# Spreading the sort of the group after next over the steps of a group, one operation at a time

## The chip, the cores and the metric

The program runs on one core of a Trainium2 chip. The metric is the device time of one launch in microseconds (us). TensorE is called PE here, VectorE DVE, ScalarE ACT, GpSimd POOL and SyncE SP. Each of them runs its own instruction stream in order; semaphores tie the streams together.

## The reference: a graph layer, an attention block and a mixture of experts

The input is `x` (3125 nodes by 256 features), 53125 edges (`src`, `dst`, `edge_weight`) and the weights of three blocks:

```python
xn = _layernorm(x)
x = x + gnn(xn, src, dst, edge_weight, W, b) + mix(xn, ...)   # mix: linear attention, 8 heads, two MLP layers
x = x + ffn(_layernorm(x), ...)                               # ffn: 16 experts, top 2 of them per token
# gnn:
msgs = edge_val[:, None] * x[edge_col]
agg = segment_sum(msgs, edge_row, num_segments=3125)
out = agg @ W.T + b
```

The change lies in the graph part alone: each edge takes the row of its `src` node, scales it by its weight and adds it to its `dst` node. Everything is float32.

## The kernel before

The kernel has five stages: norm of `x` with keys and a projection of every node written to the DRAM tensor `y_rows` (to about 170 us of the span); the edges, in 13 groups (to about 862 us); the dense attention block; the routing of tokens to experts; and the experts. The change touches the second stage.

**A group.** The edges lie in 416 columns of 128 partitions, so 13 groups (`NG`) of `GE` = 32 columns, 4096 edges each. The 3125 nodes are 25 bins (`BINS`) of 128. A group's edges are first sorted by bin, which gives `GT` = 32 tiles of 128 edges; then POOL gathers the tile's 128 rows of `y_rows` by an indirect DMA for each tile (`gather`, L582); then a group is added up in `STEPS` = 56 steps. Steps 0 to 31 are the tiles (variable `t`). Steps 32 to 55 (variable `b`, from 0 to 23) are the 24 borders between bins, where a tile belongs to two of them. Below they are called row steps and border steps, and a step number counts through both, so step 35 is `b == 3`.

**A step.** DVE makes a one-hot matrix `hot` for the step four further on (`LEAD` = 4; `hot_row` L1064, `hot_cross` L1069); PE multiplies it by the gathered rows into PSUM (L733, L748, two matmul instructions a step); DVE adds the result to `agg` (`evict_row` L1076 at each row step; `evict_pair` L1082 for two border steps at once). An eviction waits for PE by the semaphore `met` and for the eviction before it by `evicted`. PE waits for `hot_ready`. A PSUM bank holds two steps, and four banks take turns. Register values that say which bin and which column a step has are loaded by `TENSOR_LOAD` instructions on DVE at steps 0 and 16 (L1091) and 28 (L1095), and on PE after step 31 (L739).

**The sort beside it.** While group g is added up, DVE and PE also sort group g+2. It is written by hand where in the steps this happens. On DVE:

- after step 2, `count_bins`: `in_bin` (L954, 128x800) and a running count over it (L958);
- after step 16, `find_places`: adds PE's prefix sums (L963), masks (L967), reduces to a place for each edge (L972) and splits the place into tile and slot (L974 to L977);
- after steps 22, 26, 35 and 43, `make_records(g+2, k)` for the quarters k = 0 to 3 (`CH` = 8 columns each): `in_tile` (L982) and three fields of `record` (L988);
- after step 55, `make_list`: copies the sorted list out of PSUM and releases POOL's gather.

On PE: `prefix` after the matmul of step 12 (L646 to L649), and `reorder(g+2, k)`, eight products of `in_slot` and `record` (L658, sixteen matmul instructions), after the matmuls of steps 28, 34, 42 and 50. A reorder waits for its records and for ACT's `in_slot` (`slot_hot`, L392 and L394), which waits for the places.

A `drain` on DVE holds the next instruction until those before it have written. The last two groups (11 and 12) have no sort beside them, since there are no groups 13 and 14.

Of the kernel before, what the change touches and what calls it, by code (L numbers as in the profile page):

```python
# [5 lines left out]
ALU = mybir.AluOpType  # L6
# [9 lines left out]
P = 128  # L16
# [6 lines left out]
def gps_layer(nc, x, src, dst, edge_weight, gnn_W, gnn_b, Wq, Wk, Wv, Wm, W1, W2, g1, b1, g2, b2,  # L23
# [42 lines left out]
    with ExitStack() as ctx:  # L66
# [553 lines left out]
        def _(pe):  # L620
# [102 lines left out]
            def add_up(g):  # L723
                h = g % 2
                pe.wait_ge(list_ready, g + 1)
                for t in range(GT):
                    n = g * STEPS + t
                    if t % GC == 0:
                        pe.wait_ge(gathered[h][t // GC], 16 * GC * (g // 2 + 1))
                    pe.wait_ge(hot_ready, n + 1)  # L730
                    if t % 2 == 0 and g * UNITS + t // 2 >= RING:
                        pe.wait_ge(evicted, evictions_before(g, t // 2))
                    pe.matmul(bank_of(g, t // 2)[:, (t % 2) * C:(t % 2 + 1) * C], hot[:, n % HOTS, :], rows[h][:, t, :],  # L733
                              start=True, stop=True).then_inc(met, 1)
                    if g + 2 < NG and t == 12:
                        prefix(g + 2)
                    if g + 2 < NG and t == 28:
                        reorder(g + 2, 0)
# [184 lines left out]
        def _(dve):  # L923
# [25 lines left out]
                last.then_inc(xn_ready, 1)  # L949

            def count_bins(g):

                dve.tensor_tensor(in_bin[:, :, :], edges_of(bin_f, g).unsqueeze(1).to_broadcast([P, BINS, GE]),  # L954
                                  iota[:, 0:BINS].unsqueeze(2).to_broadcast([P, BINS, GE]), ALU.is_equal)
                dve.drain()
                flat = in_bin[:, :, :].rearrange("p b c -> p (b c)")
                dve.tensor_tensor_scan(count[:, 1:1 + BINS * GE], flat, flat, 0.0, ALU.add, ALU.max).then_inc(counts_ready, 1)  # L958

            def find_places(g):  # L960
                dve.wait_ge(prefix_ready, g + 1)
                places = count[:, 1:1 + BINS * GE].rearrange("p (b c) -> p b c", c=GE)
                dve.scalar_tensor_tensor(places, cross_before.unsqueeze(2).to_broadcast([P, BINS, GE]), -1.0, places,  # L963
                                         ALU.add, ALU.add)
                dve.tensor_copy(ends[:, :], ends_col)
                dve.drain()
                dve.tensor_tensor(places, places, in_bin[:, :, :], ALU.mult)  # L967

                dve.tensor_scalar(meets[:, :], tile_start[:, :], ends[:, 0:1], None, ALU.is_ge)
                dve.drain()  # L970
                with nc.allow_low_precision(reason="each sum is one whole number and zeros"):
                    dve.tensor_reduce(place_i[:, 0, :], places.rearrange("p b c -> p c b"), AX, ALU.add)  # L972
                dve.drain()
# [5 lines left out]
            def make_records(g, k):  # L979
                own = slice(k * CH, (k + 1) * CH)  # L980
                dve.drain()
                dve.tensor_tensor(in_tile[:, :, :], place_i[:, 1, own].unsqueeze(2).to_broadcast([P, CH, GT]),  # L982
                                  iota[:, 0:GT].unsqueeze(1).to_broadcast([P, CH, GT]), ALU.is_equal)
                dve.drain()
                if g * CHUNKS + k >= 2:
                    dve.wait_ge(reordered, g * CHUNKS + k - 1)
                for f in range(FIELDS):
                    last = dve.tensor_tensor(record[k % 2][:, :, f, :], in_tile[:, :, :],  # L988
                                             edges_of(edge[:, f, :], g, k).unsqueeze(2).to_broadcast([P, CH, GT]), ALU.mult)
                last.then_inc(record_ready, 1)  # L990

            def make_list(g):
                h = g % 2
# [84 lines left out]
            def evict_pair(g, a):  # L1078
# [2 lines left out]
                dve.wait_ge(evicted, g * EVICTS + GT + a)  # L1081
                dve.tensor_tensor(own, bank_of(g, GT // 2 + a), own, ALU.add).then_inc(evicted, 1)  # L1082

            def add_up(g):
                h = g % 2
                if g == 0:
# [2 lines left out]
                for t in range(GT):  # L1089
# [357 lines left out]
```

## Time and profile before

| | us |
|---|---|
| median of 3 runs | 1557.48 (1555.85 to 1558.01) |
| the profiled execution, its own time | 1554.42 |
| its span in the trace | 1552.6 |
| PE busy | 1207.1 (78%) |
| DVE busy | 960.4 (62%) |
| POOL busy | 574.9 (37%) |
| ACT busy | 357.6 (23%) |
| granted PE clock over the span | 0.919 of full speed |

The groups with a sort take 54.4 to 54.9 us each once the pipeline runs (groups 2 to 10); group 0 takes 66.5, group 1 57.0, and groups 11 and 12 together 73.3. Shares over the whole span mix five stages; what the change can move is read inside a group, from the order of DVE's and PE's instructions in time and from what each idle stretch ended with.
### The profile page before, as it was taken

To read this page: it belongs to the slowest core of one execution; us is meant where nothing else is said; L and a number is where in the kernel's file an instruction comes from. 1 tells how busy PE (TensorE), PEld (TensorE's weight loads), DVE (VectorE), ACT (ScalarE), POOL (GpSimd) and SP (SyncE) were. 2 spreads that over 40 slices of the span, in tenths; PEclk is the share of its full clock that TensorE was granted. 3 is DMA by queue.
4 is the path that set the end of the run, shared out by engine and by line. 5 is a ranking of instruction groups with operands and counts; after the bars stand their busy time and mean duration, and the time that the engine had idled before them with its cause. 6 is when DMAs were issued, how large, how long until landed. Compare 5 with 4: busy or idle time off the path is not lost.

```text
span 1552.6 us, 24067 instructions
## 1 busy us (share of the span) xinstructions
PE 1207.1 (78%) x7172; PEld 1010.1 (65%) x7172; DVE 960.4 (62%) x2681; ACT 357.6 (23%) x881; POOL 574.9 (37%) x587
## 2 busy tenths in 40 slices
PE   0589776776677677677789999999239999999990
PEld 0466455654565465455544888998229999999990
DVE  2962388888888888888989565544752222222225
ACT  0455231132033113203300343334111111111110
POOL 1420477657447545644752000000033333333320
PEclk9889987998999899899899999999559999999995
DMA  3211233323223222322321000000058999999967
GB/s 118 67 35 34 71 104 104 94 79 92 66 68 101 68 69 82 89 65 69 104 69 43 1 1 17 17 17 17 15 180 292 332 334 331 336 331 332 335 219 254
DMA packets 118265, 196.07 MB, mean 126 GB/s; under 512 B 13421, under 2 KB 67499, under 8 KB 118187
## 3 DMA queue, kind: packets, MB, share of 16 engines
q1 hardware_dynamic: 92074, 123.82, 24.0%
q0 software_dynamic: 26112, 71.34, 14.8%
q8 instruction: 33, 0.54, 0.1%
q14 instruction: 46, 0.37, 0.1%
HBM read 177.12 MB, written 17.99 MB: 126 GB/s over the span
## 4 chain that ended last, share of the span: by engine, by line
PE 58%; DVE 22%; issue 6%; DVEq 6%; DMA 3%; POOL 2%; SPq 2%; ACT 1%; ACTq 0%; POOLq 0%
PE psum L891 15%; PE psum L733 8%; PE psum L901 7%; PE psum L748 6%; PE psum L799 6%; PE psum L658 5%; DVE agg L1076 4%; PE psum L807 3%; DVE agg L1082 2%; DVE record L988 2%; PE psum L679 2%; POOL arena L582 2%; DVE in_tile L982 2%; DVE hot L1064 2%; DVEq L1091 1%
## 5 line engine op out<-in xcount | busy, mean ns | idle before, releaser
L582 POOL DMA_INDIRECT arena<-y_rows,gather_i x416 | 403.0, 969 | 334.3 <-DVEq L1011 131.5
L733 PE MATMUL psum<-arena,hot 128*128 128x256 f32 x832 | 265.8, 461 | 142.1 <-DVE hot L1064 83.2
L733 PEld LDWEIGHTS psum<-arena,hot 128*128 128x128 f32 x832 | 169.1, 224 | 228.5 <-DVE hot L1064 126.3
L392 ACT ACTIVATE in_slot<-iota,place_f 128x128 f32<-128x128 f32 x416 | 126.9, 387 | 450.8 <-DVE place_f L977 398.9
L748 PE MATMUL psum<-arena,hot 128*128 x624 | 161.8, 395 | 38.5 <-DVE hot L1069 35.1
L1076 DVE TENSOR_TENSOR agg<-psum,agg 128x256 f32 x416 | 175.9, 423 | 18.2 <-PE psum L733 17.2
L891 PEld LDWEIGHTS psum<-arena 128*128 128x128 f32 x1536 | 181.1, 194 | 4.9 <-issue 2.5
L891 PE MATMUL psum<-arena 128*128 128x128 f32 x1536 | 181.6, 277 | 1.9 <-DVE arena L1373 1.9
L1380 DVE TENSOR_TENSOR arena<-psum,arena 128x512 f32<-128x512 f32 x64 | 44.3, 692 | 202.8 <-PE psum L891 202.8
L748 PEld LDWEIGHTS psum<-arena,hot 128*128 128x128 f32 x624 | 109.0, 190 | 80.7 <-issue 70.9
L1064 DVE TENSOR_SCALAR hot<-iota,node_in_bin,weight 128x128 f32<-128x128 f32 x416 | 145.1, 354 | 24.3 <-issue 24.2
L605 POOL DMA_INDIRECT chosen_rows<-arena,back_at x64 | 63.2, 987 | 219.7 <-DVE arena L1387 215.0
L595 POOL TENSOR_TENSOR xnT<-xnT,token 128x1600 bf16<-128x1600 bf16 x2 | 10.5, 5271 | 302.2 <-DVE xnT L1349 302.2
L1082 DVE TENSOR_TENSOR agg<-psum,agg 128x512 f32<-128x512 f32 x156 | 106.5, 682 | 20.4 <-PE psum L748 20.2
L658 PE MATMUL psum<-record,in_slot 128*128 128x96 f32 x832 | 107.3, 285 | 13.2 <-DVE record L988 13.2
L524 ACT ACTIVATE arena<-psum 128x512 f32<-128x512 f32 x64 | 38.2, 597 | 335.0 <-PE psum L891 335.0
L658 PEld LDWEIGHTS psum<-record,in_slot 128*128 128x128 f32 x832 | 105.0, 201 | 15.9 <-DVE record L988 13.6
L1069 DVE TENSOR_SCALAR hot<-iota_all,node,weight 128x128 f32<-128x128 f32 x312 | 97.5, 349 | 8.2 <-issue 8.1
L901 PE MATMUL psum<-arena 128*128 128x256 f32 x384 | 90.9, 380 | 0.0
L901 PEld LDWEIGHTS psum<-arena 128*128 128x128 f32 x384 | 69.3, 191 | 7.3
L600 POOL DMA_INDIRECT xnT<-n_rows,token_of x64 | 62.0, 969 | 28.7 <-issue 18.9
L988 DVE TENSOR_TENSOR record<-in_tile,edge 128x256 f32<-128x256 f32 x156 | 64.6, 470 | 3.9
(199 smaller groups left out, 1608.3 us busy)
## 6 DMA issues: line engine op xcount, KB each, us to landing
arena<-in_L_ffn_w_dram SPq DMA_DIRECT2D x144, 512.0 KB, 5.7
xnT<-in_L_ffn_w_dram SPq DMA_DIRECT2D x48, 512.0 KB
arena<-y_rows,gather_i POOLq DMA_INDIRECT x416, 2.8
arena<-chosen_rows SPq DMA_DIRECT2D x8, 640.0 KB, 9.1
agg<-in_x_dram SPq DMA_DIRECT2D x4, 640.0 KB, 11.1
y_rows<-arena SPq DMA_DIRECT2D x4, 640.0 KB, 3.4
n_rows<-arena SPq DMA_DIRECT2D x4, 640.0 KB
out_dram<-agg SPq DMA_DIRECT2D x4, 640.0 KB
```

Of the source, the lines that this page charges most:

```text
L392: act.activation(in_slot[k % 2][:, c, :], iota[:, :], ACT.Abs, bias=place_f[:, k * CH + c:k * CH + c + 1])
L582: pool.indirect_dma_start(rows[h][:, t, :], None, y_rows, bass.IndirectOffsetOnAxis(ap=gather_i[h][:, t:t + 1], axis=0)).then_inc(gathered ...
L658: last = pe.matmul(in_order, in_slot[k % 2][:, c, :], record[k % 2][:, c, :, :].rearrange("p f t -> p (f t)"), start=(k == 0 and c == 0), ...
L733: pe.matmul(bank_of(g, t // 2)[:, (t % 2) * C:(t % 2 + 1) * C], hot[:, n % HOTS, :], rows[h][:, t, :], start=True, stop=True).then_inc(met, 1)
L748: pe.matmul(bank_of(g, unit)[:, (b % 2) * C:(b % 2 + 1) * C], hot[:, n % HOTS, :], rows[h][:, bass.ds(row_of[b], 1), :].rearrange("p t c - ...
L891: last = pe.matmul(bank[b][:, m * P:(m + 1) * P], w[s][:, k * EH + m * P:k * EH + (m + 1) * P], e_xT[:, h, k * P:(k + 1) * P], start=(k == ...
L901: last = pe.matmul(bank[6 + h][:, 0:C], e_hid[:, h, k * P:(k + 1) * P], e_w3[s][:, k * C:(k + 1) * C], start=(k == 0), stop=(k == EHC - 1))
L988: last = dve.tensor_tensor(record[k % 2][:, :, f, :], in_tile[:, :, :], edges_of(edge[:, f, :], g, k).unsqueeze(2).to_broadcast([P, CH, GT ...
L1064: dve.tensor_scalar(hot[:, n % HOTS, :], iota[:, :], node_in_bin[g % 2][:, t:t + 1], weight[g % 2][:, t:t + 1], ALU.is_equal, ALU.mult).th ...
L1069: dve.tensor_scalar(hot[:, n % HOTS, :], iota_all[:, (b + 1) * P:(b + 2) * P], node[g % 2][:, bass.ds(col, 1)], weight[g % 2][:, bass.ds(c ...
L1076: dve.tensor_tensor(own, bank_of(g, t // 2)[:, (t % 2) * C:(t % 2 + 1) * C], own, ALU.add).then_inc(evicted, 1)
L1082: dve.tensor_tensor(own, bank_of(g, GT // 2 + a), own, ALU.add).then_inc(evicted, 1)
```

## The change

The operations of the sort are the same, and so are their number, shapes and drains. They are cut into seven kinds of pieces, and each piece is issued after a step of its own, in `sort_beside(g, step)`. PE's `prefix` moves from step 12 to step 10.

```diff
-                    if g + 2 < NG and t == 12:
+                    if g + 2 < NG and t == 10:
                         prefix(g + 2)
...
-            def count_bins(g):
-
+            def mark_bins(g):
                 dve.tensor_tensor(in_bin[:, :, :], edges_of(bin_f, g).unsqueeze(1).to_broadcast([P, BINS, GE]),
                                   iota[:, 0:BINS].unsqueeze(2).to_broadcast([P, BINS, GE]), ALU.is_equal)
-                dve.drain()
+
+            def count_marks(g):
                 flat = in_bin[:, :, :].rearrange("p b c -> p (b c)")
+                dve.drain()
                 dve.tensor_tensor_scan(count[:, 1:1 + BINS * GE], flat, flat, 0.0, ALU.add, ALU.max).then_inc(counts_ready, 1)
...
+            def add_prefix(g):
                 dve.wait_ge(prefix_ready, g + 1)
...
+            def make_field(g, k, f):
+                if f == 0:
+                    dve.drain()
+                    if g * CHUNKS + k >= 2:
+                        dve.wait_ge(reordered, g * CHUNKS + k - 1)
+                last = dve.tensor_tensor(record[k % 2][:, :, f, :], in_tile[:, :, :],
+                                         edges_of(edge[:, f, :], g, k).unsqueeze(2).to_broadcast([P, CH, GT]), ALU.mult)
+                if f == FIELDS - 1:
+                    last.then_inc(record_ready, 1)
...
+            def sort_beside(g, step):
+                if step == 1:
+                    mark_bins(g)
+                if step == 3:
+                    count_marks(g)
+                if step == 13:
+                    add_prefix(g)
+                if step == 15:
+                    mask_places(g)
+                if step == 17:
+                    sum_places(g)
+                if step == 19:
+                    split_places(g)
+                for k, first in enumerate((20, 25, 34, 42)):
+                    if step == first:
+                        mark_tiles(g, k)
+                    if first < step <= first + FIELDS:
+                        make_field(g, k, step - first - 1)
...
                     if g + 2 < NG:
-                        if t == 2:
-                            count_bins(g + 2)
-                        if t == 16:
-                            find_places(g + 2)
-                        if t in (22, 26):
-                            make_records(g + 2, (t - 22) // 4)
+                        sort_beside(g + 2, t)
...
-                    if g + 2 < NG and b in (3, 11):
-                        make_records(g + 2, 2 + b // 8)
+                    if g + 2 < NG:
+                        sort_beside(g + 2, GT + b)
```

`mask_places`, `sum_places` and `split_places` hold the rest of `find_places` in its old order, each with the drain that stood in front of it; `mark_tiles` holds the drain and the `in_tile` operation of `make_records`.

In the rows below, `hot` is the one-hot matrix, `agg<-psum,agg` an eviction, and ISA an instruction of the sequencer alone.

**DVE, around step 16.** Before, the load of step 16 stands behind an eviction, and all of `find_places` behind the eviction of step 16:

```order
L1076 ISA
L1076 TENSOR_TENSOR agg<-psum,agg 128x256
L1091 TENSOR_LOAD bin_of
L1064 TENSOR_SCALAR hot<-iota,node_in_bin,weight 128x128
L1076 ISA
L1076 TENSOR_TENSOR agg<-psum,agg 128x256
L963 SCALAR_TENSOR_TENSOR count<-psum,count 128x800
L965 COPY ends<-psum 25x1
L967 TENSOR_TENSOR count<-count,in_bin 128x800
L969 TENSOR_SCALAR meets<-tile_start,ends 25x32
L972 TENSOR_REDUCE place_i<-count 128x32
L974 TENSOR_SCALAR place_i<-place_i 128x32
```

Now the same place, from the eviction of step 15 on:

```order
L1099 TENSOR_TENSOR agg<-psum,agg 128x256
L971 TENSOR_TENSOR count<-count,in_bin 128x800
L972 TENSOR_SCALAR meets<-tile_start,ends 25x32
L1133 TENSOR_LOAD bin_of
L1087 TENSOR_SCALAR hot<-iota,node_in_bin,weight 128x128
L1099 ISA
L1099 TENSOR_TENSOR agg<-psum,agg 128x256
L1087 TENSOR_SCALAR hot<-iota,node_in_bin,weight 128x128
L1099 ISA
L1099 TENSOR_TENSOR agg<-psum,agg 128x256
L977 TENSOR_REDUCE place_i<-count 128x32
```

The masking operation has moved ahead of the load, the prefix addition two steps further ahead, and the reduction one step behind it.

**DVE, around the load of step 28.** Before, the three fields of quarter 1, a one-hot matrix and an eviction stand ahead of it:

```order
L982 TENSOR_TENSOR in_tile<-place_i,iota 128x256
L988 TENSOR_TENSOR record<-in_tile,edge 128x8x32 x3
L1064 TENSOR_SCALAR hot<-iota,node_in_bin,weight 128x128
L1076 ISA
L1076 TENSOR_TENSOR agg<-psum,agg 128x256
L1095 TENSOR_LOAD cross_col
```

Now the second field stands right ahead of it, and the third behind the step:

```order
L1005 TENSOR_TENSOR record<-in_tile,edge 128x8x32
L1087 TENSOR_SCALAR hot<-iota,node_in_bin,weight 128x128
L1099 ISA
L1099 TENSOR_TENSOR agg<-psum,agg 128x256
L1005 TENSOR_TENSOR record<-in_tile,edge 128x8x32
L1137 TENSOR_LOAD cross_col
L1092 ISA
L1092 TENSOR_SCALAR hot<-iota_all,node,weight 128x128
L1099 ISA
L1099 TENSOR_TENSOR agg<-psum,agg 128x256
L1005 TENSOR_TENSOR record<-in_tile,edge 128x8x32
```

Two of the three fields stay ahead of the load, with the step 27 between them.

**DVE, border steps 34 to 36 (b = 2 to 4), quarter 2.** Here `in_tile` and the fields stand one by one:

```order
L997 TENSOR_TENSOR in_tile<-place_i,iota 128x256
L1092 ISA
L1092 TENSOR_SCALAR hot<-iota_all,node,weight 128x128
L1105 TENSOR_TENSOR agg<-psum,agg 128x512
L1005 TENSOR_TENSOR record<-in_tile,edge 128x8x32
L1092 ISA
L1092 TENSOR_SCALAR hot<-iota_all,node,weight 128x128
L1005 TENSOR_TENSOR record<-in_tile,edge 128x8x32
```

Before, they stood as one row of four operations behind the eviction of step 35, as the block in front of the load above does. On PE only `prefix` has moved, by two steps.

## Rows read from the trace of the kernel before

**Rows 1.** The chain of work that ended last, the page: shares by engine.

```profile
PE 58%; DVE 22%; issue 6%; DVEq 6%; DMA 3%; POOL 2%; SPq 2%; ACT 1%; ACTq 0%; POOLq 0%
```

**Rows 2.** Windows, group 2, groups 11 with 12: length, busy us, PEclk, DMA.

```profile
297.50:351.90 54.40, 39.67 (x186) 30.29 (x186) 48.32 (x138) 13.90 (x36) 31.00 (x32) 0.91 0.26 78
...
789.10:862.40 73.30, 64.32 (x216) 33.97 (x216) 66.83 (x196) 0.00 (x0) 30.50 (x32) 1.00 0.20 58
```

**Rows 3.** DVE by line, groups 2 to 10: count | busy, mean ns | idle before.

```profile
L1076 DVE TENSOR_TENSOR agg<-psum,agg 128x256 f32 x288 | 121.7, 423 | 5.4 <-PE psum L733 4.6 <-issue 0.5 <-PE psum L748 0.2
L1064 DVE TENSOR_SCALAR hot<-iota,node_in_bin,weight 128x128 f32<-128x128 f32 x288 | 100.0, 352 | 18.1 <-issue 18.1
L1082 DVE TENSOR_TENSOR agg<-psum,agg 128x512 f32<-128x512 f32 x108 | 73.8, 683 | 16.5 <-PE psum L748 16.5
```

**Rows 4.** DVE in time, group 5, step 15 to find_places: start, us, operation.

```profile
475.88 0.42 DVE L1076 TENSOR_TENSOR agg<-psum,agg 128x256 f32 x1
477.05 0.34 DVE L1064 TENSOR_SCALAR hot<-iota,node_in_bin,weight 128x128 f32<-128x128 f32 x1 [0.75 <-issue]
...
478.76 0.99 DVE L967 TENSOR_TENSOR count<-count,in_bin 128x800 f32<-128x800 f32 x1
```

**Rows 5.** DVE in time, step 28's load, group 5; then group 12.

```profile
490.71 1.10 DVE L988 TENSOR_TENSOR record<-in_tile,edge 128x256 f32<-128x256 f32 x3
491.73 0.34 DVE L1064 TENSOR_SCALAR hot<-iota,node_in_bin,weight 128x128 f32<-128x128 f32 x1
491.98 0.41 DVE L1076 TENSOR_TENSOR agg<-psum,agg 128x256 f32 x1
492.82 0.43 DVE L1069 TENSOR_SCALAR hot<-iota_all,node,weight 128x128 f32<-128x128 f32 x1 [0.42 <-issue]
...
847.10 0.34 DVE L1069 TENSOR_SCALAR hot<-iota_all,node,weight 128x128 f32<-128x128 f32 x1 [1.36 <-issue]
```

**Rows 6.** PE in time, group 5, steps 40 to 47 with reorder 2.

```profile
500.63 1.80 PE L748 MATMUL psum<-arena,hot 128*128 x6 [1.10 <-DVE hot L1069]
502.27 1.92 PE L658 MATMUL psum<-record,in_slot 128*128 128x96 f32 x16
504.03 2.35 PE L748 MATMUL psum<-arena,hot 128*128 x10
```

**Rows 7.** DVE in time, group 5, steps 35 to 43.

```profile
498.62 0.43 DVE L982 TENSOR_TENSOR in_tile<-place_i,iota 128x256 f32<-128x256 int32 x1
499.12 1.09 DVE L988 TENSOR_TENSOR record<-in_tile,edge 128x256 f32<-128x256 f32 x3
...
501.76 0.68 DVE L1082 TENSOR_TENSOR agg<-psum,agg 128x512 f32<-128x512 f32 x1
...
502.88 0.68 DVE L1082 TENSOR_TENSOR agg<-psum,agg 128x512 f32<-128x512 f32 x1
...
504.69 0.69 DVE L1082 TENSOR_TENSOR agg<-psum,agg 128x512 f32<-128x512 f32 x1 [0.63 <-PE psum L748]
```

**Rows 8.** DVE in time, group 5, one row step with nothing beside it.

```profile
488.77 0.34 DVE L1064 TENSOR_SCALAR hot<-iota,node_in_bin,weight 128x128 f32<-128x128 f32 x1
489.06 0.42 DVE L1076 TENSOR_TENSOR agg<-psum,agg 128x256 f32 x1
```

**Rows 9.** ACT in time, group 5: in_slot of quarters 0 and 1.

```profile
482.14 2.44 ACT L392 ACTIVATE in_slot<-iota,place_f 128x128 f32<-128x128 f32 x8 [36.02 <-DVE place_f L977]
...
485.62 2.43 ACT L392 ACTIVATE in_slot<-iota,place_f 128x128 f32<-128x128 f32 x8
```

**Rows 10.** PE in time, group 0, step 28.

```profile
213.69 0.70 PE L733 MATMUL psum<-arena,hot 128*128 128x256 f32 x2 [1.26 <-DMA arena<-y_rows,gather_i]
```

**Rows 11.** Windows: group 0, then group 5 at steps 5 to 9 and 28 to 43.

```profile
196.00:202.00 6.00, 4.53 (x12) 3.03 (x10) 3.51 (x10) 0.00 (x0) 4.64 (x5) 0.50 0.36 109
469.00:472.00 3.00, 2.72 (x6) 2.19 (x7) 3.00 (x11) 0.00 (x0) 2.10 (x3) 0.50 0.35 104
...
491.00:503.00 12.00, 9.73 (x56) 7.87 (x56) 10.66 (x32) 7.01 (x18) 8.52 (x9) 1.00 0.34 105
```

More of the change, by code:

```diff
@@ L949, in x_norm @@
                 last.then_inc(xn_ready, 1)
-            def count_bins(g):
+            def mark_bins(g):
                 dve.tensor_tensor(in_bin[:, :, :], edges_of(bin_f, g).unsqueeze(1).to_broadcast([P, BINS, GE]),
                                   iota[:, 0:BINS].unsqueeze(2).to_broadcast([P, BINS, GE]), ALU.is_equal)
+            def count_marks(g):
+                flat = in_bin[:, :, :].rearrange("p b c -> p (b c)")
                 dve.drain()
-                flat = in_bin[:, :, :].rearrange("p b c -> p (b c)")
                 dve.tensor_tensor_scan(count[:, 1:1 + BINS * GE], flat, flat, 0.0, ALU.add, ALU.max).then_inc(counts_ready, 1)
-            def find_places(g):
+            places = count[:, 1:1 + BINS * GE].rearrange("p (b c) -> p b c", c=GE)
+            def add_prefix(g):
                 dve.wait_ge(prefix_ready, g + 1)
-                places = count[:, 1:1 + BINS * GE].rearrange("p (b c) -> p b c", c=GE)
                 dve.scalar_tensor_tensor(places, cross_before.unsqueeze(2).to_broadcast([P, BINS, GE]), -1.0, places,
@@ L965, in find_places, with mask_places @@
                 dve.tensor_copy(ends[:, :], ends_col)
+            def mask_places(g):
                 dve.drain()
@@ L969, in find_places, with sum_places @@
                 dve.tensor_scalar(meets[:, :], tile_start[:, :], ends[:, 0:1], None, ALU.is_ge)
+            def sum_places(g):
                 dve.drain()
@@ L972, in find_places, with split_places @@
                     dve.tensor_reduce(place_i[:, 0, :], places.rearrange("p b c -> p c b"), AX, ALU.add)
+            def split_places(g):
                 dve.drain()
@@ L977, in find_places, with count_bins, mark_tiles @@
                 dve.tensor_scalar(place_f[:, :], place_i[:, 2, :], -1.0, None, ALU.mult).then_inc(places_ready, 1)
-            def make_records(g, k):
+            def count_bins(g):
+                mark_bins(g)
+                count_marks(g)
+            def find_places(g):
+                for part in (add_prefix, mask_places, sum_places, split_places):
+                    part(g)
+            def mark_tiles(g, k):
                 own = slice(k * CH, (k + 1) * CH)
@@ L983, in make_records @@
                                   iota[:, 0:GT].unsqueeze(1).to_broadcast([P, CH, GT]), ALU.is_equal)
-                dve.drain()
-                if g * CHUNKS + k >= 2:
-                    dve.wait_ge(reordered, g * CHUNKS + k - 1)
+            def make_field(g, k, f):
[7 more added lines that the diff above has]
+                    last.then_inc(record_ready, 1)
+            def make_records(g, k):
+                mark_tiles(g, k)
                 for f in range(FIELDS):
-                    last = dve.tensor_tensor(record[k % 2][:, :, f, :], in_tile[:, :, :],
-                                             edges_of(edge[:, f, :], g, k).unsqueeze(2).to_broadcast([P, CH, GT]), ALU.mult)
-                last.then_inc(record_ready, 1)
+                    make_field(g, k, f)
             def make_list(g):
@@ L1082, in evict_pair @@
                 dve.tensor_tensor(own, bank_of(g, GT // 2 + a), own, ALU.add).then_inc(evicted, 1)
+            def sort_beside(g, step):
+                if step == 1:
+                    mark_bins(g)
+                if step == 3:
+                    count_marks(g)
+                if step == 13:
[8 more added lines that the diff above has]
+                    if step == first:
+                        mark_tiles(g, k)
+                    if first < step <= first + FIELDS:
+                        make_field(g, k, step - first - 1)
             def add_up(g):
```

## The prediction

> **What bounds the kernel now.** I read the chain of work first, then the windows by group, then DVE's idle time by line, then DVE and PE in time. The chain [rows 1] names PE for 58% and DVE for 22%, but over five stages; it doesn't say which is short inside a group. The windows do [rows 2]: the nine groups 2 to 10 lie between 297.50 and 789.10, 54.6 us each, and in the one shown DVE is busy 48.3 and PE 39.7. DVE is the full engine. What a faster order can win is therefore DVE's idle time and nothing of its work. In those nine groups [rows 3] it idles 16.5 us in border evictions and 4.8 in row evictions, each time for PE, that is 1.83 and 0.53 us a group; and 18.1 us (2.0 a group) ahead of a one-hot matrix for "issue", which is the two L1091 loads. The sum is some 4.4 us a group, and of that the load at step 0 stands behind `make_list`, which isn't touched. Groups 11 and 12, without a sort, take 36.65 each, so the sort costs 18 us a group, nearly all of it DVE's own work that stays.
>
> PE's idle stretches beside `find_places` look like the large thing but cost nothing themselves: PE catches up, a step taking it 0.47 us (5 steps in 2.35 [rows 6]) and DVE 0.63 (0.34 from eviction to one-hot, 0.29 back [rows 5, 8]). They cost only through what is late after them.
>
> **The load of step 16.** It follows an eviction that starts at 475.88; the next one-hot matrix starts at 477.05 [rows 4], 1.17 later instead of 0.34, so 0.83 us are exposed and the load takes about 1.1. In the new order the masking operation (0.99) and a short one stand ahead of it, and the sequencer can take the load while they run. If it needs about 0.1 to hand over the two, the one-hot matrix starts 1.3 after the masking operation's start, where the engine is free at 1.04: 0.26 exposed. Gain 0.57. The bounds are 0 (the load waits for the engine) and 0.83.
>
> **The load of step 28.** Before, the block starts at 490.71 and the next one-hot matrix at 492.82, though the engine could take it at 492.32: 0.50 exposed. In group 12, with no block ahead, the row shows 1.36 idle [rows 5]. The block thus gives the sequencer a lead of 0.9. After, only one field, a step and another field stand behind the last drain. If the sequencer's hand-over sets the load's start, it starts about 0.35 after the first field and the matrix follows 2.14 after it, the engine being free at 1.28: 0.86 exposed, a loss of 0.36. If it was the number of instructions ahead in the queue, nothing is lost. I take 0.17, halfway. Both loads together: +0.40 a group.
>
> **The border evictions.** Before, the four operations of a quarter hold DVE from 498.62 on (0.50 to the first field, then 0.34 for each, with 0.18 for the drain in front 1.7 in all), PE has no one-hot matrix for 1.10 us, runs three steps, then reorders for 1.76 (502.27 to the next start at 504.03) [rows 6, 7]. The eviction of steps 42 and 43 comes 1.81 after the one before it, not 1.12, and waits 0.63. The reorder itself would fit: eight border steps with a quarter's operations cost DVE 4 x 1.11 (two evictions are 1.12 apart) + 1.7 = 6.1, and PE 8 x 0.47 + 1.76 = 5.5. The wait comes from PE's being stopped just before. I lay out the new order at each reorder, counting from the start of the one-hot matrix of the reorder's step. PE: the matrix done and read at 0.4, the step to 1.07 (0.67 for a single one), reorder to 2.83, next step to 3.3, eviction possible at 3.5. DVE reaches that eviction at:
> - quarter 1 (step 34): two row steps 1.27, two border steps 1.11, matrix and drain 0.44, `in_tile` 0.34, matrix 0.26 = 3.42, wait 0.1;
> - quarter 2 (step 42): 2.22 for four border steps, then the same 1.04 = 3.26, wait 0.24;
> - quarter 3 (step 50): no operation is left in these steps, 2.73, wait 0.75.
>
> Sum 1.09 against 1.83: gain 0.74. Bounds: 0, if the waits return elsewhere, and 1.83.
>
> **The row evictions.** Their 0.53 us a group fall in stretches after a block in which PE runs at half clock: 2.72 busy in 3.00 for three steps at a clock of 0.50 (1.2 GHz) [rows 11], slower than DVE's 0.63. The clock had been 1.00 (2.4 GHz), and fell after PE had stood idle beside the counting. PE is now never left without a matrix for longer than one operation and its drain take, where `find_places` held DVE by eight in a row, but the idle stretch around `make_list` is left, and tiles come spaced out. I take half: 0.25, bounds -1.5 (below) and 0.53.
>
> **Instruction overlap.** From one-hot to eviction DVE takes 0.29 in a plain row step, but 0.25 in a step that follows a block [rows 5, 8], since an eviction waits for the end of the one before it and the block has covered that. Fourteen row steps now have an operation ahead of the next matrix instead of four: 10 x 0.04, of which two stand beside loads. 0.25; bounds 0 and 0.4.
>
> **What is not changed.** Same operations and the same drains; a drain behind an eviction costs 0.1 as one behind a short operation does, so 0, with bounds of ±0.3 a group. No DMA moves. ACT now starts its `in_slot` at the end of step 19 instead of 16 and needs 3.5 a quarter (482.14 to 485.62 [rows 9]). PE wants quarter 0 after step 28, when DVE is at step 24: five steps with four operations, 3.2 + 1.7 = 4.9 after the places. It is in time by 1.4, and quarter 1 by 3. The prefix wait at step 13 stands behind a PE step whose matrix was made at step 6. Behind that wait would queue the one-hot matrices of all later steps, so it would hurt if it came; seven steps cover it. `make_list` closes the group as before, so POOL's gathers (31 us busy of 54.5 [rows 2]) keep their cover.
>
> **The sum.** 0.40 + 0.74 + 0.25 + 0.25 = 1.64 us a group, in groups 1 to 10: 16.4. In group 0 the rows come late: PE waits for a gather until 213.69, at step 28 [rows 10], so the row steps gain nothing, and I count the border term alone, 0.7. Together 17.1 off the profiled execution's 1554.4, which gives 1537.3; the shown median stands 3.1 above that execution, so 1540.4.
>
> **Rivals.**
> - *The waits only move* (the new places of the fields leave PE late all the same), or the load of step 28 is exposed at 0.86 or more. For it: reorder 3 keeps its wait in my own layout. Then 0.6 to 0.9 a group stays, 8 us: 1549.
> - *All waits for PE go.* 2.36 + 0.57 + 0.25 = 3.2 in ten groups and 1.8 in group 0, 34 us: 1524. Against it: reorder 3, where nothing delays DVE.
> - *No change*, within 0.2% (3.1 us, about what a measurement can tell here): drains behind evictions eat what the loads give.
> - *Slower: PE's clock.* In group 0, with the tiles paced by the gathers, the clock stood at 0.50 from 196 to 202 [rows 11]. Steps 13 to 19 will be paced similarly by DVE, one in 8.7 / 7 = 1.25 us. If the clock is low when reorders 0 and 1 run, each takes 1.76 longer, and six steps between them 0.3 more than DVE needs: 5.3, less 1.1 of cover, less the 1.64 gained, is 2.6 a group lost, 26 us: 1583. It decides from an extra wait of 1.64, about one reorder at half clock in every group. Against it: border steps with stops of 1.1 us before each reorder keep 1.00 over 491 to 503 [rows 11].
>
> The Trainium skill ("TensorE: Matmul & The Clock Gate", "A second HAM failure mode: psum-queue depth-cycling") tells of a kernel in which short idles between groups of matmuls made the clock oscillate; by that rule many small gaps would be no better than few long ones, and the time would be that of the rival named last. The border steps here speak against it, the gather-paced stretch for it.
>
> **How the numbers follow.** Forecast 0.57 (its own range 1533 to 1546), waits only move 0.19, all go 0.10, no change 0.07, slower 0.07. Faster by over 0.2%: 0.57 + 0.19 + 0.10 = 0.86; same 0.07; slower 0.07. The range 1529 to 1553 holds the first two cases and parts of the next.
>
> **What the changed profile would show.** Groups 2 to 10 of about 53.0 us with DVE busy still 48.3. The idle time ahead of the one-hot matrix at step 16 at 0.2 instead of 0.75, that of step 28 at 0.4 to 0.8. Border evictions waiting 1.1 a group, mostly at step 51. PE with no idle stretch over 2 us but the one around `make_list`. I am wrong if DVE's busy time or its drains grow, if the eviction waits stay near 2.4 a group, if the clock in steps 28 to 36 is below 1.00, or if PE waits for ACT or records at a reorder.

## The result, and the profile after

| | before | after |
|---|---|---|
| median of 10 runs, us | 1556.9 | 1546.06 |
| the profiled execution's span, us | 1552.6 | 1543.0 |
| start of group 0 | 174.0 | 174.9 |
| group 0 | 66.5 | 68.8 |
| group 1 | 57.0 | 54.3 |
| groups 2 to 10, mean | 54.6 | 53.5 |
| granted PE clock over the span | 0.919 | 0.906 |

The changed kernel takes 0.9939 of the time before (95% interval 0.9924 to 0.9953), 9.5 us less. 17.1 were forecast. In the spans the difference is 9.6 us: 0.9 lost ahead of group 0, 2.3 lost in group 0, 2.8 won in group 1, 10.5 won in groups 2 to 10 (1.17 each, where 1.64 was forecast), 0.4 lost behind them. Group times here and below come from one profiled execution of each kernel; that of the changed kernel was one of its two fastest (1544.75; its ten runs lie between 1544.75 and 1552.75).

The groups no longer take the same time. These are the windows of groups 2, 4, 7 and 10 of the changed kernel (length, busy us of PE, its weight loads, DVE, ACT and POOL, PEclk, DMA), which answer to [rows 2]:

```profile
297.90:349.90 52.00, 42.09 (x186) 29.25 (x186) 47.76 (x138) 13.90 (x36) 32.64 (x32) 0.90 0.27 82
...
404.10:457.80 53.70, 44.45 (x186) 31.98 (x186) 47.66 (x137) 13.91 (x36) 32.16 (x32) 0.84 0.27 79
...
563.60:619.00 55.40, 46.41 (x186) 33.68 (x186) 47.94 (x137) 13.91 (x36) 32.88 (x32) 0.82 0.26 76
...
725.90:779.10 53.20, 42.16 (x186) 29.72 (x186) 47.74 (x138) 13.91 (x36) 32.61 (x32) 0.90 0.27 80
```

DVE's work is the same within 0.3 us in all four. The clock differs, but its mean over a group doesn't give the length: groups 2 and 10 both have 0.90 and take 52.0 and 53.2. What gives it is how long DVE waits for PE before its row evictions: nothing in group 2, 1.84 us in group 4, 2.77 in group 7, 0.91 in group 10. With these waits taken off, all nine groups are 51.9 to 52.7 long. Before, the nine lay between 54.4 and 54.9.

DVE by line over groups 2 to 10 of the changed kernel, against [rows 3] (L1099 is L1076 before, L1087 is L1064, L1105 is L1082, L1092 is L1069):

```profile
L1099 DVE TENSOR_TENSOR agg<-psum,agg 128x256 f32 x288 | 121.4, 421 | 11.8 <-PE psum L733 10.5 <-issue 1.4
L1087 DVE TENSOR_SCALAR hot<-iota,node_in_bin,weight 128x128 f32<-128x128 f32 x288 | 99.6, 351 | 12.0 <-issue 11.3
L1105 DVE TENSOR_TENSOR agg<-psum,agg 128x512 f32<-128x512 f32 x108 | 74.2, 687 | 6.3 <-PE psum L748 5.9
L1092 DVE TENSOR_SCALAR hot<-iota_all,node,weight 128x128 f32<-128x128 f32 x216 | 72.7, 360 | 6.9 <-issue 6.9
```

Three of the four went about as laid out: the border evictions wait 6.3 us instead of 16.5, the matrices of the row steps 12.0 instead of 18.1, those of the border steps 6.9 instead of 4.7, for which this is the line of the kernel before:

```profile
L1069 DVE TENSOR_SCALAR hot<-iota_all,node,weight 128x128 f32<-128x128 f32 x216 | 67.5, 349 | 4.7 <-issue 4.5
```

The row evictions went the other way, 11.8 instead of 5.4.

**The loads.** DVE in time in group 2, steps 15 and 16, against [rows 4]:

```profile
313.13 0.99 DVE L971 TENSOR_TENSOR count<-count,in_bin 128x800 f32<-128x800 f32 x1
314.04 0.22 DVE L972 TENSOR_SCALAR meets<-tile_start,ends 25x32 f32<-25x32 f32 x1
314.34 0.35 DVE L1087 TENSOR_SCALAR hot<-iota,node_in_bin,weight 128x128 f32<-128x128 f32 x1
```

The matrix of step 16 starts 1.21 after the masking operation, with less than 0.1 us of idle time: the load runs under the two. And steps 26 to 28, against [rows 5]:

```profile
325.56 0.43 DVE L1005 TENSOR_TENSOR record<-in_tile,edge 128x256 f32<-128x256 f32 x1
325.91 0.34 DVE L1087 TENSOR_SCALAR hot<-iota,node_in_bin,weight 128x128 f32<-128x128 f32 x1
326.16 0.42 DVE L1099 TENSOR_TENSOR agg<-psum,agg 128x256 f32 x1
326.50 0.42 DVE L1005 TENSOR_TENSOR record<-in_tile,edge 128x256 f32<-128x256 f32 x1
327.64 0.35 DVE L1092 TENSOR_SCALAR hot<-iota_all,node,weight 128x128 f32<-128x128 f32 x1 [0.73 <-issue]
```

The matrix follows 2.08 after the first field (2.11 before), with one field less in between, so 0.73 idle instead of 0.42. In the trace the load itself starts 0.32 after that field (0.35 before) and takes 1.60 us both times. It is tied to the field behind the last drain, not to the number of instructions ahead.

**The border steps.** The only wait left in group 2 is the one at reorder 3 [rows 7]:

```profile
343.54 0.69 DVE L1105 TENSOR_TENSOR agg<-psum,agg 128x512 f32<-128x512 f32 x1
344.14 0.60 DVE L1092 TENSOR_SCALAR hot<-iota_all,node,weight 128x128 f32<-128x128 f32 x2
345.35 0.69 DVE L1105 TENSOR_TENSOR agg<-psum,agg 128x512 f32<-128x512 f32 x1 [0.61 <-PE psum L748]
```

**The row steps.** PE in time, group 4, steps 4 to 10 (0 to 3 ran while the group before ended), then DVE's evictions at steps 10 and 12:

```profile
405.75 4.15 PE L733 MATMUL psum<-arena,hot 128*128 128x256 f32 x8 [2.84 <-issue]
411.00 2.90 PE L733 MATMUL psum<-arena,hot 128*128 128x256 f32 x6 [1.10 <-issue]
```

```profile
416.12 0.42 DVE L1099 TENSOR_TENSOR agg<-psum,agg 128x256 f32 x1 [1.45 <-PE psum L733]
417.82 0.42 DVE L1099 TENSOR_TENSOR agg<-psum,agg 128x256 f32 x1 [0.39 <-PE psum L733]
```

And the clock there, in the first 12 us of group 4 and of group 2:

```profile
404.00:416.00 12.00, 9.12 (x25) 6.57 (x26) 9.32 (x24) 0.00 (x0) 9.21 (x9) 0.55 0.28 80
...
298.00:310.00 12.00, 8.81 (x33) 5.68 (x33) 10.69 (x28) 0.00 (x0) 9.30 (x9) 0.86 0.27 82
```

In both groups PE had stood idle 2.8 us beside `make_list`. In group 4 the clock averages 0.55, near its lower level of 0.50, over the 12 us; PE does 25 matmuls in them, in group 2 it does 33. Eight of them take 4.15 us, 1.04 a step, against DVE's 0.63. `prefix`, which now stands behind step 10, comes on top. (A row eviction waits for both steps of its bank, so the one of step 10 waits for the matmuls of step 11, behind `prefix`.) DVE then waits 1.45 and 0.39. In five groups of the nine (3, 4, 6, 7 and 8) these two waits, or a pair like them, stand at steps 10 and 12; group 10 has one of 0.91 at step 10. The kernel before had half clock in the row steps too, but at most 0.9 us of waits for PE in a group.

Group 7 has the dearest case: the clock is low again at step 28, and reorder 0 takes 3.73 instead of 2.02.

```profile
592.15 3.73 PE L658 MATMUL psum<-record,in_slot 128*128 128x96 f32 x16
```

```profile
596.82 0.42 DVE L1099 TENSOR_TENSOR agg<-psum,agg 128x256 f32 x1 [1.87 <-PE psum L733]
```

**Group 0.** PE at step 28, against [rows 10]:

```profile
216.17 0.70 PE L733 MATMUL psum<-arena,hot 128*128 128x256 f32 x2 [1.67 <-DMA arena<-y_rows,gather_i]
216.80 0.40 PE L656 MATMUL psum<-meets,ones 25*128 25x32 f32 x2
217.13 3.38 PE L658 MATMUL psum<-record,in_slot 128*128 128x96 f32 x16
```

The rows come 2.5 us later than before, and the reorder behind them runs at half clock, 3.38 instead of 2.03. Of the 2.5, 0.9 is the later start of the group; the other 1.6 goes with slower gathers on POOL, told under the last heading. But group 0 is not steady between executions, as the kernels of the experiments show. It took 66.9 to 70.3 in the one execution traced of each. Two of them keep the blocks in its row steps, and they took 68.2 and 70.3. The start of the group moved between 174.0 and 176.0, though nothing ahead of it was changed. So one execution of the kernel before, at 66.5, doesn't show that the 2.3 us come from the new order.

### The profile page after: what moved, and what is told of

It reads as the page before. It is cut to its first block, busy times and chain, and to the rows that moved or that the text cites. A ratio compares the mean times of both kernels' runs of the same rounds, so it can differ in the third digit from the quotient of the medians.

```text
span 1543.0 us, 24067 instructions
## 1 busy us (share of the span) xinstructions
PE 1246.6 (81%) x7172; PEld 1018.0 (66%) x7172; DVE 955.8 (62%) x2681; ACT 357.7 (23%) x881; POOL 589.8 (38%) x587
## 4 chain that ended last, share of the span: by engine, by line
PE 57%; DVE 20%; issue 10%; DVEq 5%; DMA 3%; POOL 2%; SPq 2%; ACT 1%; ACTq 0%; POOLq 0%
PE psum L891 15%; PE psum L733 10%; PE psum L901 7%; PE psum L799 6%; PE psum L658 4%; DVE agg L1099 4%; PE psum L748 4%; PE psum L807 3%; DVE hot L1092 3%; DVE agg L1105 2%; PE psum L679 2%; POOL arena L582 2%; DVE hot L1087 1%; DVE record L1005 1%; PE psum L628 1%
## 5 line engine op out<-in xcount | busy, mean ns | idle before, releaser
L582 POOL DMA_INDIRECT arena<-y_rows,gather_i x416 | 417.9, 1005 | 309.1 <-issue 122.8
L733 PE MATMUL psum<-arena,hot 128*128 128x256 f32 x832 | 291.4, 490 | 111.4 <-issue 63.9
L1099 DVE TENSOR_TENSOR agg<-psum,agg 128x256 f32 x416 | 175.5, 422 | 28.3 <-PE psum L733 26.8
L748 PE MATMUL psum<-arena,hot 128*128 x624 | 168.0, 400 | 21.2 <-DVE hot L1092 20.9
L1087 DVE TENSOR_SCALAR hot<-iota,node_in_bin,weight 128x128 f32<-128x128 f32 x416 | 144.6, 353 | 16.9 <-issue 15.7
L595 POOL TENSOR_TENSOR xnT<-xnT,token 128x1600 bf16<-128x1600 bf16 x2 | 10.5, 5270 | 302.4 <-DVE xnT L1386 302.4
L658 PE MATMUL psum<-record,in_slot 128*128 128x96 f32 x832 | 110.9, 291 | 12.7 <-DVE record L1005 12.7
L658 PEld LDWEIGHTS psum<-record,in_slot 128*128 128x128 f32 x832 | 108.4, 207 | 15.4 <-DVE record L1005 13.1
L1105 DVE TENSOR_TENSOR agg<-psum,agg 128x512 f32<-128x512 f32 x156 | 107.1, 687 | 8.0 <-PE psum L748 7.3
L1092 DVE TENSOR_SCALAR hot<-iota_all,node,weight 128x128 f32<-128x128 f32 x312 | 104.1, 360 | 11.1 <-issue 11.0
L1005 DVE TENSOR_TENSOR record<-in_tile,edge 128x256 f32<-128x256 f32 x156 | 71.8, 468 | 4.6
L901 PEld LDWEIGHTS psum<-arena 128*128 128x128 f32 x384 | 69.2, 190 | 7.4
```

The costliest lines, as they stand in the source:

```text
L582: pool.indirect_dma_start(rows[h][:, t, :], None, y_rows, bass.IndirectOffsetOnAxis(ap=gather_i[h][:, t:t + 1], axis=0)).then_inc(gathered ...
L658: last = pe.matmul(in_order, in_slot[k % 2][:, c, :], record[k % 2][:, c, :, :].rearrange("p f t -> p (f t)"), start=(k == 0 and c == 0), ...
L748: pe.matmul(bank_of(g, unit)[:, (b % 2) * C:(b % 2 + 1) * C], hot[:, n % HOTS, :], rows[h][:, bass.ds(row_of[b], 1), :].rearrange("p t c - ...
L901: last = pe.matmul(bank[6 + h][:, 0:C], e_hid[:, h, k * P:(k + 1) * P], e_w3[s][:, k * C:(k + 1) * C], start=(k == 0), stop=(k == EHC - 1))
L1087: dve.tensor_scalar(hot[:, n % HOTS, :], iota[:, :], node_in_bin[g % 2][:, t:t + 1], weight[g % 2][:, t:t + 1], ALU.is_equal, ALU.mult).th ...
L1092: dve.tensor_scalar(hot[:, n % HOTS, :], iota_all[:, (b + 1) * P:(b + 2) * P], node[g % 2][:, bass.ds(col, 1)], weight[g % 2][:, bass.ds(c ...
```

## The experiments

My theory after the result: the order on DVE wins 2.6 us a group (54.6 to 52.0, as groups 2 and 5 show), and half clock on PE takes back 1.5 of it on average (53.5 against 52.0). Rivals: the spread of the groups comes from POOL or DMA, or from the spread order itself. Each of the eight kernels ran beside the kernel before on the same chip: the first three below and the one with the masking operation on one chip, the others on another. Kernels are therefore compared by their ratios to the kernel before.

### Only the border steps

```diff
+                if step == 2:
+                    count_bins(g)
+                if step == 16:
+                    find_places(g)
+                if step in (22, 26):
+                    make_records(g, (step - 22) // 4)
+                for k, first in ((2, 34), (3, 42)):
```

> The kernel before with only quarters 2 and 3 of the records taken apart (steps 34 to 37 and 42 to 45); counting, places and quarters 0 and 1 stay blocks, prefix stays at step 12. Theory (the gain is in the border evictions, the loss in PE's half clock in the row steps): border waits fall from 1.83 to about 0.65 a group, row waits stay at 0.53, groups 2 to 10 of 53.4 us each, 1.2 x 11 = 13 us less than the kernel before, about 1543, a little faster than the change as a whole. Rival (the spread of the group times comes from something else, such as POOL's slower gathers, and will be there as soon as anything is spread): group times spread between 52 and 55 here too, 1548 to 1552.

Measured 1549.94 (1543.34 to 1554.49), ratio 0.995 (0.9928 to 0.9973). Groups 2 to 10 take 53.75 on average, between 53.0 and 54.6. DVE by line over them:

```profile
L1099 DVE TENSOR_TENSOR agg<-psum,agg 128x256 f32 x288 | 121.9, 423 | 5.9 <-PE psum L733 5.2 <-issue 0.3 <-PE psum L748 0.2
...
L1105 DVE TENSOR_TENSOR agg<-psum,agg 128x512 f32<-128x512 f32 x108 | 74.1, 686 | 6.9 <-PE psum L748 6.2
```

The border waits fell from 1.83 to 0.77 a group, the row waits stayed (0.66 against 0.60). The groups are 0.87 shorter (53.75 against 54.62), about what the border waits lost, as the theory has it. But the total is 7 us above what I expected and lies in the rival's range of 1548 to 1552; the runs are wide. The groups spread less than the rival wanted, and more than mine did. By itself it decides little on the clock, but it shows one thing that my theory didn't have:

```profile
299.80:311.80 12.00, 8.65 (x26) 6.48 (x26) 10.33 (x26) 0.00 (x0) 9.02 (x9) 0.57 0.30 89
```

This is the start of group 2. In five of the nine groups the clock is 0.57 to 0.72 over the first 12 us, where the kernel before has 0.86 in all nine, although the row steps stand in their blocks here. So the low clock at a group's start doesn't need the spread row steps; what brings it down there stays open.

### Only the row steps

```diff
-                for k, first in enumerate((20, 25, 34, 42)):
+                for k, first in enumerate((20, 25)):
...
+                if step in (35, 43):
+                    make_records(g, 2 + (step - 35) // 8)
```

> The changed kernel with quarters 2 and 3 put back into blocks behind steps 35 and 43; all row steps as changed. Theory: the load at step 16 is hidden (-0.7 a group), overlap -0.3, the load at step 28 more exposed (+0.3), row waits for PE at half clock +0.7, group 0 +2 to 3 us: the sum is about nil, 1554 to 1560 (no change against the kernel before). Reorder 0 runs at half clock (over 3 us) in some of the groups and never in others, and these groups are the long ones. Rival (the clock is not what costs): -0.7 a group, 1549.

Measured 1558.19, ratio 1.001 (0.9999 to 1.0022): nothing won. Group 0 takes 69.2, groups 2 to 10 54.6.

```profile
L1099 DVE TENSOR_TENSOR agg<-psum,agg 128x256 f32 x288 | 121.3, 421 | 13.6 <-PE psum L733 12.3 <-issue 1.0 <-PE psum L748 0.3
L1087 DVE TENSOR_SCALAR hot<-iota,node_in_bin,weight 128x128 f32<-128x128 f32 x288 | 100.1, 353 | 12.0 <-issue 11.3
L1105 DVE TENSOR_TENSOR agg<-psum,agg 128x512 f32<-128x512 f32 x108 | 74.2, 687 | 14.7 <-PE psum L748 14.6
```

The load's gain is there (12.0 for 18.1), and the row evictions eat it (13.6 for 5.4). As the chip's clock stands, all that the change wins on balance comes from the border steps. One thing was not as I had written: no group from 1 on had its reorder 0 at half clock here, and the waits of 0.9 to 1.8 us in the early row steps alone made up the loss. (The expectations place them at steps 5 to 9; counted out in the trace they stand at 10 and 12.)

### Matmuls that only keep PE at work

```diff
+            FILL = {5: 3, 7: 5, 17: 3, 19: 4, 21: 5, 23: 2, **{t: 1 for t in (24, 25, 26, 27)}}
...
+                if 1 <= g < NG - 1:
+                    for _ in range(7):
+                        pe.matmul(bank[4][:, 0:P], ident[:, :], iota[:, :], start=True, stop=True)
...
+                        for _ in range(FILL.get(t, 0)):
+                            pe.matmul(bank[4][:, 0:P], ident[:, :], iota[:, :], start=True, stop=True)
```

> The changed kernel with matmuls added on PE whose result (128x128, in an unused bank) nobody reads: 7 ahead of a group, 3 to 5 where DVE does a long operation of the sort, 1 or 2 at steps 23 to 27. They only keep PE at work where it would stand idle. Theory: the granted clock stays at 1.00 in the row steps, the row waits of 1.3 us a group go, every group of 2 to 10 takes 51.9 to 52.2 us, 1.4 x 10 = 14 us less than the changed kernel, about 1532. Rival (the waits have another cause, such as POOL or the order of the instructions): the same 53.5 us a group or more, since PE has more to do: 1546 to 1556.

Measured 1532.14 (1530.98 to 1533.21), ratio 0.9838 (0.982 to 0.9855). The stretch from group 2 to group 10, and DVE's row evictions in it:

```profile
297.00:766.00 469.00, 417.48 (x2266) 321.42 (x2267) 429.60 (x1232) 125.14 (x324) 292.02 (x287) 1.00 0.28 82
```

```profile
L1107 DVE TENSOR_TENSOR agg<-psum,agg 128x256 f32 x288 | 121.1, 421 | 1.4 <-issue 0.8 <-PE psum L738 0.6
```

PE has more to do and everything ends sooner: the clock is 1.00 throughout these groups, the row waits fall from 11.8 to 1.4 us, and the nine groups take 52.3 on average (51.9 to 52.8), 1.2 less than in the changed kernel. That is 10.6 of the 13.8 us between the two spans; 1.9 more lie in group 0, whose length isn't steady, and the rest ahead of the groups and behind them. POOL is as busy as in the changed kernel (292.0 against 292.6 us), so it is not what spread the groups. This is the experiment that shows the clock as the cause of the row waits: its time is 14 us below the changed kernel's (16 by the ratios) and was expected there.

### The same in the kernel before

```diff
+            FILL = {6: 8, 20: 12, 26: 5}
```

> The kernel before (blocks) with matmuls added on PE whose result nobody reads: 7 ahead of a group, 8, 12 and 5 at steps 6, 20 and 26, where a block of DVE leaves PE idle. Theory (half clock costs the blocks little, and the spread order much): the row waits of 0.53 us a group go, the border waits of 1.83 stay, 54.0 us a group, 5 to 6 us less than the kernel before, about 1550. Rival (PE's clock is worth the same in both orders, 14 us): about 1542.

Measured 1553.09 (1548.94 to 1554.59), ratio 0.9962 (0.9947 to 0.9977), 5.9 us less by the ratio. The clock from group 2 to group 10 is 0.99, the groups take 54.06 on average instead of 54.6, and the border waits stay (in group 4 0.79, 0.61 and 0.61).

```profile
299.00:789.00 490.00, 412.97 (x2274) 318.11 (x2273) 436.76 (x1249) 125.14 (x324) 283.53 (x288) 0.99 0.26 78
```

So the two orders don't pay alike: with the clock held up, blocks take 54.06 a group and the spread order 52.3. The order is worth 1.8 a group, of which the chip's clock left 1.17.

### Which of the added matmuls count

At the group's start (7 ahead, steps 5 and 7) alone:

```diff
+            FILL = {5: 3, 7: 5}
```

> The changed kernel with the added matmuls ahead of the group and at steps 5 and 7 alone. Theory: the waits of 1.45 and 0.39 us that stand at steps 5 to 9 in five of nine groups go, which is most of the loss; half clock between steps 13 and 28 stays possible and costs little unless it reaches reorder 0. About 1536. Rival (the later stretch is the dear one): 1542 or more.

Measured 1534.44 (1531.48 to 1534.94), ratio 0.9851 (0.9837 to 0.9866). And at steps 17 to 27 alone:

```diff
+            FILL = {17: 3, 19: 4, 21: 5, 23: 2, **{t: 1 for t in (24, 25, 26, 27)}}
```

> The changed kernel with the added matmuls at steps 17 to 27 alone. Theory: the waits at steps 5 to 9 stay, only those at reorder 0 (one group in nine, 1.87 us, and group 0) go: about 1543. Rival: 1536, if the later stretch is the dear one.

Measured 1545.49 (1543.92 to 1546.39), ratio 0.9921 (0.9908 to 0.9934). The start of a group is where the loss was. DVE's row evictions, first with the matmuls at the start, then with the later ones:

```profile
L1107 DVE TENSOR_TENSOR agg<-psum,agg 128x256 f32 x288 | 121.1, 421 | 1.4 <-PE psum L738 0.8 <-issue 0.5
```

```profile
L1107 DVE TENSOR_TENSOR agg<-psum,agg 128x256 f32 x288 | 121.0, 420 | 10.0 <-PE psum L738 8.9 <-issue 0.7 <-PE psum L756 0.3
```

The second kernel also compares groups with each other, with the same instructions in each: groups 4 and 6 have a clock of 0.97, no row waits, and take 51.9; groups 5, 7 and 10 have 0.87, 1.83 us of row waits, and take 53.9 to 54.4. The window over groups 2 to 10 of the first kernel:

```profile
297.00:766.00 469.00, 395.42 (x1941) 284.25 (x1941) 429.01 (x1230) 125.15 (x324) 294.69 (x288) 0.95 0.28 82
```

Its clock is still low for a tenth of the time (0.95), in the later row steps, and its groups take 52.2 all the same. There the sort's operations hold DVE at about a step in 1.2 us (8.2 us from the eviction of step 12 to that of step 19), and PE keeps up at half clock. In these kernels half clock costs where DVE runs at 0.63 a step (steps 4 to 12) or where a reorder meets it.

### The masking operation behind the load

```diff
-                if step == 15:
+                if step == 16:
                     mask_places(g)
```

> The changed kernel with the masking operation after step 16 instead of 15, so that the load of step 16 stands behind an eviction again. Theory: the idle time ahead of the one-hot matrix of step 16 is back at 0.75 us, 0.7 x 11 = 7 us more than the changed kernel, 1553. Rival (the load was never worth anything): within 2 us of 1546.

Measured 1553.69 (1551.08 to 1557.0), ratio 0.998 (0.9969 to 0.9991), that is 6 us more than the changed kernel by the ratios.

```profile
L1087 DVE TENSOR_SCALAR hot<-iota,node_in_bin,weight 128x128 f32<-128x128 f32 x288 | 99.7, 351 | 18.0 <-issue 18.0
```

The 18 us are back (18.1 in the kernel before, 12.0 in the changed one): what hid the load is the masking operation ahead of it.

### A version that beats both

The added matmuls stay, but 10 of them stand ahead of a group and none at step 5; `mark_bins` is issued ahead of the load of step 0; quarter 1 has its second and third field both at step 27, ahead of the load of step 28.

```diff
+                    if t == 0 and g + 2 < NG:
+                        mark_bins(g + 2)
                     if t % MLOAD == 0:
...
+                    steps = [first + 1, first + 2, first + 2 if k == 1 else first + 3]
```

> The changed kernel with the added matmuls (10 ahead of a group, none at step 5), with mark_bins ahead of the load of step 0, and with quarter 1's second and third field both ahead of the load of step 28. The bin operation of 0.98 us should hide as much of the load of step 0 (1.25 us idle to about 0.3), the added field 0.34 of the load of step 28 (0.73 to about 0.4). That is 1.2 us a group less than with the added matmuls alone: 1532 - 13 = 1519. Rival (the load of step 0 is held up by make_list's last drain in any order, or the marked bins only delay PE's first matrices): 1528 to 1532.

Measured 1521.81 (1520.74 to 1523.82), ratio 0.9771 (0.9758 to 0.9783). Groups 2 to 10 take 51.3. DVE in time at the start of group 2, and the matrices by line over the nine groups:

```profile
296.72 0.99 DVE L961 TENSOR_TENSOR in_bin<-edge_i,iota 128x800 f32<-128x800 f32 x1
297.89 0.34 DVE L1095 TENSOR_SCALAR hot<-iota,node_in_bin,weight 128x128 f32<-128x128 f32 x1 [0.18 <-issue]
```

```profile
L1095 DVE TENSOR_SCALAR hot<-iota,node_in_bin,weight 128x128 f32<-128x128 f32 x288 | 97.0, 342 | 2.4 <-issue 1.6
...
L1100 DVE TENSOR_SCALAR hot<-iota_all,node,weight 128x128 f32<-128x128 f32 x216 | 71.3, 352 | 4.7 <-issue 4.5
```

The load of step 0 shows 0.18 us idle instead of 1.25. Over the two evictions and the two matrices DVE idles 1.7 us a group, against 3.0 with the added matmuls alone and 4.1 in the changed kernel; the largest piece is the wait at reorder 3.

## Why the prediction was right in direction and too large by 7.6 us

- **DVE bounds the group; the gain is in its idle time.** Right in the main: of the 1.17 us won a group, 0.7 is idle time and 0.5 is busy time (48.3 to 47.8), which I had said would stay. Nor is the sort's 18 us "nearly all" DVE's own work: groups 11 and 12 have 33.4 busy each, so it is 14.9 of the 18.
- **The load of step 16**, 0.57: it won 0.68, and putting the operation back behind the load took it away.
- **The load of step 28**, -0.17 between two readings: it lost 0.24 by line (0.31 at the load itself). The dearer of my two readings, that the hand-over sets the load's start, was the right one.
- **The border evictions**, 0.74: they won 1.13 (16.5 to 6.3 us over nine groups). The wait at reorder 3 is there (0.61, laid out at 0.75), that at reorder 1 is gone, and of that at reorder 2 0.1 to 0.2 is left in three of the nine groups.
- **Instruction overlap**, 0.25: the busy time fell by 0.5. It fell with the row steps spread (47.9) and not with the border steps alone (48.4), as the term has it.
- **The row evictions**, +0.25: this is the step that failed. I took the half clock of [rows 11] for something that follows a long stop of DVE and would halve with it. It costs 1.31 a group now and cost 0.60 before: -0.71. With the clock held at 1.00 it is 0.16. The error, 0.96 a group, is 8.6 us over groups 2 to 10, more than the whole shortfall of 7.6; the border evictions and the busy time gave part of it back. The terms together come to 1.33 a group; the 1.17 measured is less because DVE's other idle time grew by 0.2.
- **Group 0**, +0.7: it lost 2.3 in the executions traced. I read [rows 10] rightly, that the gathers set the row steps there, and then took them for fixed. They got slower, and the reorder behind them ran at half clock. But that reorder ran at half clock with the old row steps too (3.73 us in the experiment with only the border steps), so how much of the 2.3 is the change's stays open.
- **Where the 7.6 us are**: 4.3 in groups 2 to 10, 3.0 in group 0, 1.3 ahead of the groups and behind them, less 1.1 that group 1 won beyond the forecast. That 9.5 of the 17.1 were still won is partly luck: a term with the wrong sign was met by others that had been put too small.
- **The rival of PE's clock** named the right mechanism and a wrong size. It put the low clock at steps 13 to 19 and on to reorders 0 and 1. It came in the first 12 us of a group, where I had not looked (0.55 to 0.73 in six of the nine), and reached reorder 0 in one group of nine and in group 0. The rule that I had weighed (the Trainium skill, "TensorE: Matmul & The Clock Gate", "A second HAM failure mode: psum-queue depth-cycling") spoke against the change. The trace agrees this far: the clock over groups 2 to 10 was 0.87 with PE's idle stretches and 1.00 with matmuls in them. It didn't turn the sign.
- **ACT, the prefix and the records were in time**, as laid out: no wait for them on PE shows in any group. Of the signs that I named, those of the two loads hold (less than 0.1 and 0.73); the border waits came lower than the 1.1 laid out (0.71), DVE's busy time fell, and the clock in steps 28 to 36 stayed at 1.00 in groups 1 to 10 but for group 7.

## What to carry to other kernels

Taking blocks apart on the engine that bounds a stage pays where another engine must be fed right after, and where a long operation can cover a register load; both can be counted from the order and a few rows. But look at what the new order does to PE's clock: it averaged 0.87 over groups 2 to 10 here instead of 0.91, and more of the low part fell where DVE was fastest. A few matmuls that nobody reads, placed where PE idles anyway, won 14 to 16 us here in the spread order (medians 1532.14 and 1546.06, ratios 0.9838 and 0.9939) and 6 in the blocks by the ratio.

## What the runs showed of the hardware that I had not expected

**POOL's gathers grew slower with the spread order.** An indirect DMA takes POOL 971 ns on average over groups 2 to 10 before, 1016 after:

```profile
L582 POOL DMA_INDIRECT arena<-y_rows,gather_i x288 | 279.5, 971 | 202.6 <-DVEq L1011 117.6 <-issue 85.0
```

```profile
L582 POOL DMA_INDIRECT arena<-y_rows,gather_i x288 | 292.6, 1016 | 179.5 <-DVEq L1034 94.5 <-issue 85.0
```

In time, POOL and DVE at the start of group 5 of the changed kernel:

```profile
459.38 0.94 POOL L582 DMA_INDIRECT arena<-y_rows,gather_i  x1 [0.30 <-issue]
460.63 1.49 POOL L582 DMA_INDIRECT arena<-y_rows,gather_i  x1 [0.30 <-issue]
462.42 0.95 POOL L582 DMA_INDIRECT arena<-y_rows,gather_i  x1 [0.30 <-issue]
463.67 1.53 POOL L582 DMA_INDIRECT arena<-y_rows,gather_i  x1 [0.30 <-issue]
```

```profile
460.32 0.98 DVE L953 TENSOR_TENSOR in_bin<-edge_i,iota 128x800 f32<-128x800 f32 x1
...
462.62 1.83 DVE L959 TENSOR_TENSOR_SCAN count<-in_bin 128x800 f32<-128x800 f32 x1
```

A gather that starts while DVE runs one of the three 800-wide operations with two inputs from SBUF ends 0.75 to 0.82 us after that operation does, so it takes longer the earlier it starts in it: 1.49 from 0.31 into the bins operation, 1.53 from 1.05 into the count, up to 1.75 from 0.07 into the masking. Over groups 2 to 10 these 27 gathers average 1.51. A gather that is already under way when such an operation starts takes 0.94 to 1.02, and 0.95 is what one takes beside the reduction (one input) or the prefix addition (one input from PSUM).

In the kernel before the same operations ran, and mostly only the count was met (1.45 to 1.81). Its bins operation started 0.33 after a gather, and the next gather came when it was all but over:

```profile
465.21 0.94 POOL L582 DMA_INDIRECT arena<-y_rows,gather_i  x1 [0.30 <-issue]
466.46 1.47 POOL L582 DMA_INDIRECT arena<-y_rows,gather_i  x1 [0.30 <-issue]
```

```profile
464.29 0.98 DVE L954 TENSOR_TENSOR in_bin<-edge_i,iota 128x800 f32<-128x800 f32 x1
465.35 1.83 DVE L958 TENSOR_TENSOR_SCAN count<-in_bin 128x800 f32<-128x800 f32 x1
```

So it is where the operations fall between the starts of two gathers that changed, not what they are. The Trainium skill ("SBUF — State Buffer", "Who interferes with whom") says that a DVE instruction with two SBUF inputs contends with a GpSimd instruction that reads SBUF and that a reduction never does; the trace agrees, 1.49 and 1.53 against 0.94. It costs nothing from group 1 on, where POOL still waits 10.5 us a group for DVE to release it (13.1 before). In group 0 it makes some 1.6 us (32 gathers at 1019 ns instead of 970). Whether that lengthens group 0 was not tried, and two kernels whose gathers average 980 ns there took 68.2 and 70.3 for it as well.

**The clock stayed low for 12 us in group 4 while PE was busy 9.1 of them**, and in group 2 it was up again within 12, after the same 2.8 us of idle time. What decides between the two these runs don't show.
